# Scan layers: state inputs and state sums issued for two pieces at a time on the tensor engine

## What is computed

```python
dt = softplus(...)                                  # per token and inner feature
A = -exp(A_log)                                     # per inner feature and state
dA = exp(dt[..., None] * A)
dBu = (dt * u)[..., None] * Bm[:, :, None, :]

def step(h, inp):
    dA_t, dBu_t, C_t = inp
    h = dA_t * h + dBu_t
    return (h, einsum('bdn,bn->bd', h, C_t))        # sum over the 16 states
y = scan(step, h0, ...) + u * D
out = y * silu(z) @ out_w.T
```

## Time and profile before

| | us |
|---|---|
| median of 3 runs | 2986.35 |
| the three runs | 2976.28, 2986.35, 2987.12 |
| the profiled execution, its own time | 2974.7 |
| its span | 2972.9 |
| scan stage of group 1 (first input to last sum) | 1807 to 2009 |
| scan stage of group 2 | 2382 to 2435.5 |
| TensorE busy, all of the span | 2699.4 (91%) |
| VectorE, ScalarE, GpSimd busy | 1657.2, 1114.7, 609.4 |

### The profile page before, as it was taken

One profiled execution on the slowest core, in us unless ns is written; L12 is line 12 of the kernel. 1 busy time (PEld: TensorE's weight loads), 2 busy tenths in 40 slices (PEclk: granted clock), 3 DMA queues, 4 the chain that ended last, 5 costly groups with the idle time before them and its releaser, 6 DMA issues. The chain is left out here.

```text
span 2972.9 us, 43154 instructions
## 1 busy us (share of the span) xinstructions
PE 2699.4 (91%) x17159; PEld 1858.4 (63%) x17159; DVE 1657.2 (56%) x3739; ACT 1114.7 (37%) x1993; POOL 609.4 (20%) x316
## 2 busy tenths in 40 slices
PE   5899999999999999689999878998996788889978
PEld 2566666666666666456767645665983367868846
DVE  5656565665656554646666555773551251067755
ACT  2343434344343432215555536641331252311123
POOL 2040403122131400000000004771001051145402
PEclk9999999999999999899999989998998989989989
DMA  4223242332323211231010001115758527653101
GB/s 155 78 72 104 75 117 74 104 96 77 100 70 107 70 48 36 86 112 46 24 45 24 1 6 37 43 36 191 259 223 277 163 79 287 226 178 133 67 14 35
DMA packets 101277, 295.48 MB, mean 99 GB/s; under 512 B 8728, under 2 KB 59110, under 8 KB 94422
## 3 DMA queue, kind: packets, MB, share of 16 engines
q1 hardware_dynamic: 97078, 283.75, 30.3%
q0 software_dynamic: 2976, 8.13, 0.8%
q10 hardware_dynamic: 1024, 0.86, 0.1%
HBM read 280.64 MB, written 11.54 MB: 98 GB/s over the span
## 5 line engine op out<-in xcount | busy, mean ns | idle before, releaser
L1904 PE MATMUL L_xattn_bank<-L_xattn_keys_tok,L_xattn_probsT 128*128 128x257 f32 x1664 | 426.1, 395 | 10.0 <-ACT L_xattn_probsT L1721 2.9
L1833 PE MATMUL L_xattn_wide<-L_xattn_keys_feat,weights_a 128*128 128x512 f32 (+2 forms) x1024 | 380.9, 515 | 2.5 <-ACT L_xattn_keys_feat L1741 1.2
L1904 PEld LDWEIGHTS L_xattn_bank<-L_xattn_keys_tok,L_xattn_probsT 128*128 128x128 f32 x1664 | 295.4, 189 | 103.8 <-issue 47.3
L1833 PEld LDWEIGHTS L_xattn_wide<-L_xattn_keys_feat,weights_a 128*128 128x128 f32 x1024 | 189.0, 190 | 153.6 <-issue 123.6
L1490 DVE COPY L_xattn_k_normed<-L_xattn_wide 128x833 f32<-128x833 f32 (+1 forms) x128 | 131.1, 1024 | 192.0 <-PE L_xattn_wide L1833 192.0
L2850 DVE TENSOR_TENSOR_SCAN L_attn_state<-L_attn_decay,L_attn_banks 128x1024 f32<-128x1024 f32 x80 | 182.7, 2286 | 70.9 <-PE L_attn_banks L3052 70.9
L1715 ACT ACTIVATE L_xattn_scores<-L_xattn_scores,L_xattn_neg_max 128x897 f32<-128x897 f32 x128 | 126.4, 1035 | 221.9 <-DVE L_xattn_neg_max L1515 221.9
L2956 POOL TENSOR_TENSOR L_attn_state<-L_attn_state,L_attn_C_rows 128x1024 f32<-128x1024 f32 x80 | 188.7, 2360 | 71.5 <-DVE L_attn_state L2850 71.4
L3052 PEld LDWEIGHTS L_attn_banks<-L_attn_B_diagonal,L_attn_dt_u_tok 128*128 128x128 f32 x1280 | 150.9, 194 | 66.1 <-issue 64.5
L1510 DVE CUSTOM_DVE_ANT_0 L_xattn_scores<-L_xattn_wide,L_xattn_mask_row 128x897 f32<-128x897 f32 x128 | 134.9, 1088 | 96.9 <-issue 96.9
L2119 DVE CUSTOM_DVE_ANT_0 L_xattn_scores<-L_xattn_banks,L_xattn_mask 128x512 f32<-128x512 f32 (+1 forms) x256 | 131.4, 570 | 92.5 <-issue 92.5
(11 more groups left out here) (519 smaller groups left out, 4715.0 us busy)
## 6 DMA issues: line engine op xcount, KB each, us to landing
L_xattn_k_scale<-L_xattn_k_scale_rows SPq DMA_DIRECT2D x128, 417.0 KB, 5.0
L_xattn_ctx_feat<-in_ctx_feat SPq DMA_DIRECT2D x24, 1601.0 KB, 10.0
L_ffn_expert_w<-in_x_L_ffn SPq DMA_DIRECT2D x16, 2056.0 KB, 8.5
L_ffn_expert_w<-in_x_L_ffn SPq DMA_DIRECT2D x17, 1024.0 KB, 5.5
L_ffn_expert_w<-in_x_L_ffn SPq DMA_DIRECT2D x15, 1028.0 KB, 5.8
L_xattn_keys_tok<-in_ctx_tok SPq DMA_DIRECT2D x8, 1536.0 KB
L_attn_C_rows<-L_attn_c_rows SPq DMA_DIRECT2D x48, 256.0 KB, 3.2
L_xattn_ctx_tok<-in_ctx_tok SPq DMA_DIRECT2D x8, 1536.0 KB
```

Source lines behind the costliest of these rows:

```text
L1833: last = nc.tensor.matmul(wide[:, 2 * h + c, 0:n], wk[:, k, p * P:(p + 1) * P], xnT[b % 2][:, k, a:a + n], start=(k == 0), stop=(k == KT - 1))
L1904: last = nc.tensor.matmul(bS[:, 0:D + 1], pT[:, c, a, :, :].rearrange("p h q -> p (h q)"), xn[b % 2][:, t, :], start=(i == 0), stop=(i == ...
```

## The change

Only the order of the tensor engine's stream changes: the loop takes pieces first and first + 1 together, both `state_input`, then both `start_y` where there are any, then both `add_state`. No instruction is added or removed, and no wait is changed.

```diff
-                for p in range(PIECES):
-                    if p + 2 < PIECES:
-                        state_input(p + 2)
-                    if p >= SPAN and p - SPAN < PC:
-                        start_y(1, p - SPAN)
-                    if ND > 1 and p == PIECES - 1:
-                        pe.wait_ge(scanned, PIECES - 1)
-                        pe.wait_ge(yz_ready, PC)
-                        for t in range(2):
-                            project_out(0, t)
-                    add_state(p)
+                for first in range(0, PIECES, 2):
+                    for p in (first, first + 1):
+                        if p + 2 < PIECES:
+                            state_input(p + 2)
+                    for p in (first, first + 1):
+                        if p >= SPAN and p - SPAN < PC:
+                            start_y(1, p - SPAN)
+                    for p in (first, first + 1):
+                        if ND > 1 and p == PIECES - 1:
+                            pe.wait_ge(scanned, PIECES - 1)
+                            pe.wait_ge(yz_ready, PC)
+                            for t in range(2):
+                                project_out(0, t)
+                        add_state(p)
```

## The result

| us | before | changed |
|---|---|---|
| first comparison: median (range), runs | 2982.43 (2976.28 to 2987.12), 5 | 2967.24 (2962.27 to 2974.15), 5 |
| ratio, 95% interval | | 0.995 (0.9928 to 0.9972) |
| second comparison, below: median (range), runs | 2981.78 (2974.97 to 2990.85), 11 | 2968.57 (2965.21 to 2973.75), 6 |
| ratio, 95% interval | | 0.9959 (0.9944 to 0.9974) |
| profiled execution, span | 2972.9 | 2972.4 |

The two stages together are 11.06 us shorter, 10.9 had been worked out, yet the two profiled spans differ by 0.5 us only: in this execution the rest of the kernel, whose code is the same, took 10.5 us more.

The account below looks back on a forecast made before the run. The tensor engine's own instruction order and shape changes were taken to bound the scan. Pairs 12.6 + older waits 0.3 - stalls 2.7 + end 0.7 = 10.9 us gained, 2986.35 to 2975.4; range 2961 to 2987 (8 in 10).

Parts of the forecast that it names:

- The gain of a pair: Tensor engine's scan stream: two pieces take 5.65 us instead of 6.00, 0.35 saved, 36 pairs giving 12.6.
- nothing at the sums: Lower bound: two sums in a row save nothing, only inputs save 0.19 a pair, leaving 5.1 us gained.
- No waits in the pair: Steady pairs run without waits; the second input has 0.8 us in hand before it needs its scan.
- single places: Spots outside the steady pairs: first pairs of both groups and pieces 32 and 33 lose 2.7 us; ends gain 0.7.
- First pair of group 1: Input 3, now directly behind input 2, must wait for scan 1: a stall of 0.87 us.
- Pieces 32 and 33: Vector engine's taking of y waits for sum 30, delaying scan 33, so input 35 stalls 1.04 us.
- End of group 2: Last product ready 9.25 us behind input 14, where sum 15 came 9.92 behind it before: 0.7 gained.
- Stages: Scan stage of group 1 shorter by 8.8 us, that of group 2 by 2.2.
- No gain in the switches: Rival: shape changes cost nothing, savings belong to their spots; only single places count, 1.7 us slower, 2988.1; chance 0.12.
- The second input waits in every pair: Rival: at `state_input(first + 3)` scan first + 1 ends late; at 2 us late, 31 slower, 3017; chance 0.04.
- Gain beyond the sum: Rival: three stalls don't appear (13 to 14 gained) or median falls to fastest run; 2961 to 2972; chance 0.24 together.
- the stated case: Whole kernel: the worked-out 10.9 us gain holds, median between 2970 and 2981 us; chance 0.60.

Follow-up runs that it names:

- second comparison: Changed kernel timed again beside the kernel before, five rounds on one chip: 2968.57 us against 2981.78, ratio 0.9959.
- experiments 3 to 5: Changed kernel plus one 8-column product per group 2 pair, between sums (stage 53.85 us) or inputs (52.59), against 50.78; then shapes alone without layers: two rounds 6.00 to 5.65.
- experiment 5: All layers left out, tensor engine alone alternating blocks without waits: two rounds 6.00 us one by one, 5.65 two by two with quarters; whole array 10.44 both ways.

## Why the prediction was right

**The gain of a pair.** 0.35 was forecast from rows of the kernel before; 0.35 was measured (6.00 to 5.65, the mean of twelve pairs), and the same in a kernel without waits. The bound "nothing at the sums" fell with experiments 3 to 5. The working leaned on places where the old order happened to issue what the new one always does; that was the strongest evidence, and its 3.77 and 1.88 held to the hundredth.

**No waits in the pair.** Forecast 0.8 us in hand for the second input. In the pair shown the two scans end at 1840.67 + 4.46 = 1845.13 and the second input is due at 1844.22 + 1.79 = 1846.01: 0.88, or 0.8 behind the handoff. No input in the steady stretch waits for a scan; from 1820 to 1990 two do, both in the single places.

**Single places.** First pair of group 1: stall 0.87 forecast, 0.85 measured. Pieces 32 and 33: 1.04 forecast, 0.96 measured. End of group 2: 9.25 forecast, 9.23 measured. Stages: 8.8 and 2.2 forecast, 8.94 and 2.12 measured. (The prediction's own terms for group 1, 30 x 0.35 + 0.10 - 0.87 - 1.04, make 8.7; with it the stages add up to its 10.9.)

**The rivals.** "No gain in the switches" did not come true: at the change from quarters to the whole array the loader stands idle until the first matmul of the new shape, 28 times in 28, and the whole-array row of experiment 5 shows that without a change there is nothing to gain. The Trainium skill (TensorE: Matmul & The Clock Gate, Part 1) has weight loads pulled ahead of matmuls in flight; by that rule the round trip would have been free, and the trace does not agree with it across a change of shape; within one shape it does (0.43 us ahead, experiment 5). "The second input waits in every pair" did not occur. "Gain beyond the sum" had two halves: the stalls did appear, so the gain in the stages stayed at the sum, but the median did fall further.

**The absolute time.** 2975.4 was forecast, 2967.24 and 2968.57 measured: inside the range, but in the 2961 to 2972 of "gain beyond the sum" (chance 0.24), not in the 2970 to 2981 of the stated case. The mechanism of the stated case held and its number for the median did not; that the range took the median in is owed to the spread allowed for the runs. The gain of 0.5% in the first comparison lies on the border of what was given 0.71, the 0.4% of the second inside it. The sum isn't what was off, the base was: it was taken from the median of three runs, 2986.35, and eleven runs have 2981.78. From there 10.9 less is 2970.9, 2.3 above the second median. The difference between the medians, 13.2 us, has an interval of 8 to 17 that holds 11; whether the 2 us over the stages are real stays open.

## What to carry to other kernels

In these kernels (fp32, full granted clock) a stream that alternates between whole-array and quarter-array (or half-array) products pays 0.35 to 0.40 us for each round trip, 0.25 around one product of 8 columns, hidden in an engine that reads as 100% busy. Look whether the first weight load of a block starts together with its first matmul instead of ahead of it, and compare with a place where the shape doesn't change. Grouping by two halves that price, giving all products one shape removes it, and is worth more where the larger products carry zeros. When work is regrouped in an in-order stream, name the few places where a consumer in another engine (here the taking of y) needed the old order: they cost 2.7 of 13.6 us in the forecast here, and laying the pairs past them gave 2.25 back.

## What the runs showed of the hardware that was not expected

Half-array shapes pay as much as quarters: 0.40 us for 64 rows x 128 columns and 0.35 for 128 rows x 64 columns, against 0.35 for 64 x 64. A sum of two quarter-array products takes 1.00 us, as long as one of four, so halving such a block by products halves nothing. And 64 small passes, four side by side, span 1.11 us where 16 passes of the whole array, with twice the multiplications, spanned 2.05.
